# Gate values as four more columns of the value product, a cross product in two row groups, a scan input in two column tiles, and new instruction orders

## The reference

```python
# 1. masked multi-head attention, 16 heads: self (causal), then against ctx, then a small MLP
x1 = layernorm(x + mha(x, x));  x2 = layernorm(x1 + mha(x1, ctx));  x = layernorm(x2 + mlp(x2))
# 2. the pair block: a gate, a cross product, an unscaled self attention
norm_X, norm_F = layernorm(ctx), layernorm(x)
attended = softmax(norm_F @ norm_X.T * scale) @ norm_X
h = gelu(attended @ fc1_w.T + fc1_b)              # 256 -> 4 channels
cross = h @ fc2_w.T + fc2_b                       # 4 -> 256 channels
n = layernorm(cross);  sa = softmax(n @ n.T * scale) @ n
x = norm_F + gamma2 * (cross + gamma1 * sa)
# 3. x = x + softmax(x @ ctx.T) @ ctx
# 4. the mix block: 8-head attention against layernorm(ctx), then a scan over positions
x = x + mha(layernorm(x), layernorm(ctx))
U = (layernorm(x) @ W_in.T + b_in) @ Bmat         # 64 scan channels
s = silu(s @ A.T) + U[t];  x = x + states @ Cmat + mod
```

## Time and profile before

| | |
|---|---|
| median of 3 runs | 4207.41 us (4206.75 to 4208.32) |
| the profiled execution | 4207.95 us, span 4206.2 us |
| PE | 4042.6 us busy (96%) |
| DVE | 3431.2 us (82%) |
| ACT | 3175.7 us (76%) |
| POOL | 2911.0 us (69%) |
| granted clock, mean | 0.989 |

### The profile page before, as it was taken

How to read it: one execution, slowest core, us unless ns; L and a number is a source line. 1 busy time by engine, 2 the same in 40 slices (tenths; PEclk the granted TensorE clock), 3 DMA queues, 4 the chain that set the end, 5 groups by cost and what they waited for, 6 DMA issues and landing times.

```text
span 4206.2 us, 112214 instructions
## 1 busy us (share of the span) xinstructions
PE 4042.6 (96%) x37547; PEld 3383.5 (80%) x37547; DVE 3431.2 (82%) x9517; ACT 3175.7 (76%) x6733; POOL 2911.0 (69%) x3172
## 2 busy tenths in 40 slices
PE   4899999999999999999999999999999999999859
PEld 3688888888888888888888888888888888888645
DVE  3688888888888888888888888888888888888634
ACT  1577887887788778877887787788778877887632
POOL 0477777777777777777777777777777777777634
PEclk9999999999999999999999999999999999999979
DMA  3000100010001100000100010101000000100037
GB/s 108 19 25 25 33 30 28 25 33 30 28 25 33 30 28 26 30 29 27 31 30 28 25 33 30 28 25 33 30 28 26 30 28 25 33 30 25 17 103 272
DMA packets 116547, 159.98 MB, mean 38 GB/s; under 512 B 11350, under 2 KB 103323, under 8 KB 111579
## 3 DMA queue, kind: packets, MB, share of 16 engines
q1 hardware_dynamic: 111626, 146.75, 11.2%
q10 hardware_dynamic: 4368, 6.17, 0.5%
HBM read 115.01 MB, written 37.88 MB: 36 GB/s over the span
## 4 chain that ended last, share of the span: by engine, by line
PE 67%; ACT 12%; POOL 7%; issue 5%; DVE 4%; DMA 0%; ACTq 0%; DVEq 0%; POOLq 0%; SPq 0%
PE bank L674 15%; PE bank L744 9%; PE bank L666 7%; PE bank L682 6%; PE bank L858 4%; PE bank L714 3%; ACT prob L992 3%; PE bank L778 3%; PE bank L693 3%; PE bank L773 2%; POOL rs_ln L1404 2%; PE bank L791 2%; POOL X L1424 2%; POOL X L1418 2%; ACT probT L1002 2%
## 5 line engine op out<-in xcount | busy, mean ns | idle before, releaser
L1158 DVE TENSOR_REDUCE mx<-bank 128x4 f32<-128x512 f32 x1280 | 837.6, 681 | 90.4 <-PE bank L714 68.6
L1169 DVE TENSOR_TENSOR prob<-bank,mx 128x512 f32<-128x512 f32 x1280 | 847.8, 679 | 54.6 <-PE bank L744 33.8
L1002 ACT ACTIVATE probT<-bank 128x512 f32<-128x512 f32 x1280 | 753.3, 600 | 158.9 <-PE bank L778 100.5
L992 ACT ACTIVATE prob<-prob 128x512 f32<-128x512 f32 x1280 | 795.6, 641 | 22.0 <-DVE prob L1169 20.9
L982 ACT ACTIVATE turned<-bank 128x512 f32<-128x512 f32 x896 | 531.9, 616 | 344.0 <-PE bank L666 223.5
L744 PE MATMUL bank<-ident,prob 128*128 128x128 f32 x5120 | 746.3, 277 | 20.3 <-DVE den L1180 6.5
L744 PEld LDWEIGHTS bank<-ident,prob 128*128 128x128 f32 x5120 | 591.3, 142 | 124.9 <-issue 36.8
L674 PE MATMUL bank<-turned,shared 128*128 128x256 f32 x2560 | 605.7, 384 | 1.8 <-ACT turned L982 1.8
L674 PEld LDWEIGHTS bank<-turned,shared 128*128 128x128 f32 x2560 | 468.3, 191 | 69.9 <-issue 14.3
L1404 POOL TENSOR_TENSOR rs_ln<-ve_ln,half 128x2 f32<-128x2 f32 x320 | 226.4, 707 | 384.9 <-DVE ve_ln L1147 384.9
L1483 POOL TENSOR_SCALAR shared<-turned,half_of 128x512 f32<-128x512 f32 x256 | 399.1, 1570 | 79.9 <-ACT turned L982 79.9
(11 more groups left out here) (242 smaller groups left out, 9047.8 us busy)
## 6 DMA issues: line engine op xcount, KB each, us to landing
shared<-in_x SPq DMA_DIRECT2D x128, 256.0 KB, 3.0
CB<-in_ctx SPq DMA_DIRECT2D x64, 256.0 KB, 3.4
CC<-in_ctx SPq DMA_DIRECT2D x64, 256.0 KB, 2.8
mod<-mod_rows SPq DMA_DIRECT2D x64, 256.0 KB, 3.3
residual<-X SPq DMA_DIRECT2D x64, 256.0 KB, 3.5
out<-turned SPq DMA_DIRECT2D x16, 1024.0 KB, 4.8
turned<-residual SPq DMA_DIRECT2D x14, 1024.0 KB, 7.3
u_turned<-us SPq DMA_DIRECT2D x64, 64.0 KB, 2.4
```

What stands on the lines that cost most here:

```text
L992: nc.scalar.activation(flat(t), flat(t), ACT.Exp, scale=SCALE[p]).then_inc(*st["act"].mark(f"exp.{b}{r}"))
L1002: nc.scalar.activation(flat(t), banks.of(f"{att}.turn.{b}{r}")[:, :], ACT.Copy).then_inc(*st["act"].mark(f"probT.{b}{r}"))
L1158: nc.vector.tensor_reduce(m[:], banks.of(f"{att}.tile.{b}{r}")[:, :].rearrange("p (h t) -> p h t", h=4), AX, ALU.max)\
L1169: nc.vector.tensor_tensor(t[:], banks.of(f"{att}.tile.{b}{r}")[:, :].rearrange("p (h t) -> p h t", h=4), maxes.of(f"{att}.max.{b}{r}")[:]. ...
```

## The change

The four gate columns go into the value product: `w_v3` gets 260 columns, of which the last four are `w_gate` scaled by the norm's gain, and the norm's shift goes into the gate's bias once at the start. The step `vx` and its copy are gone; `mix_in.v` is done one round earlier (lag 4), into two banks, and `vp3` has two buffers. DVE divides the probabilities themselves by their sum before `pT1` turns them (`part1`), in place of the two small steps after `av1`. `av1` exchanges its operands, so that its result has the four gate channels on partitions 0 to 3 and 32 to 35; the Gelu reads it from the bank, adds the bias and writes `y5T` directly. `yT` and its copy are gone. `cross` is two products of 32 rows, one per sequence, in two row groups and two banks; ACT copies them with two instructions. `mix_out.u` puts the sequences in two column tiles of 64; SP stores it with two DMAs. PROGRAM and BANKS are written anew for all engines.

The core of the diff (in the kernel after, lines stand 7 to 11 further down):

```diff
-    "pe": """ mix_att.scores.00@6 ctx_att.turn.12@4 ctx_att.values.01@4 ...
+    "pe": """ ctx_att.values.00@4 ctx_att.values.03@4 mix_att.scores.00@6 pair.cross@5 ...
...
-    pair.sc2:2 pair.pT2:6 pair.av:6 real.x4T:2 real.ccT:4 real.screal:4 real.pTreal:4 real.av:5 real.h5T:5
+    ffn.fc2:2 pair.CT:0 pair.FT:2 mix_in.v0:0 mix_in.v1:6 pair.sc1:2 pair.pT1:2 pair.av1:7 pair.cross0:4
...
-        vp3 = sb("vp3", [128, G, D])
+        vp3 = [sb(f"vp3_{n}", [128, G, D + 4]) for n in range(2)]
...
-                def vx(g):
+                def v3(g):
...
+                    took = [banks.claim(f"mix_in.v{b}", mix_in["act"], "v") for b in range(G)]
...
-                            last = nc.tensor.matmul(t[:, b * 4:b * 4 + 4], trn["NXT"][:, a, b * S:(b + 1) * S],
-                                                    w_gate[:, a, :], start=(a == 0), stop=(a == DH - 1))
+                            last = nc.tensor.matmul(t[:, 0:D + 4], trn["HCT"][:, a, b * S:(b + 1) * S], w_v3[:, a, :],
+                                                    start=(a == 0), stop=(a == DH - 1))
...
-                        last = nc.tensor.matmul(t[:, b * 4:b * 4 + 4], pct["1"][:, b, :], vxs[:, b, :], start=True, stop=True)
+                        last = nc.tensor.matmul(t[32 * b:32 * b + 4, 0:S], vp3[g % 2][:, b, D:D + 4], pct["1"][:, b, :], start=True, stop=True)
...
-                        last = nc.tensor.transpose(t[:, b * S:(b + 1) * S], y5[:, b, :], ident[:])
-                    last.then_inc(*pair["pe"].mark("yT"))
...
-                        last = nc.tensor.matmul(t[:, b * D:(b + 1) * D], y5T[:, b, :], w_cross[:], start=True, stop=True)
+                        rows_ = slice(32 * b, 32 * b + 32)
+                        last = nc.tensor.matmul(t[:, 0:D], y5T[rows_, :], w_cross[rows_, :], start=True, stop=True)
...
-                        last = nc.tensor.matmul(t[:, 0:W], w_u[:, a, :], trn["H6T"][:, a, :], start=(a == 0), stop=(a == DH - 1))
+                        for b in range(G):
+                            last = nc.tensor.matmul(t[NS * b:NS * b + NS, 0:S], w_u[:, a, :], trn["H6T"][:, a, b * S:(b + 1) * S],
+                                                    start=(a == 0), stop=(a == DH - 1))
...
-                    nc.scalar.activation(y5[:, :, 0:4], a4[:], ACT.Gelu).then_inc(*pair["act"].mark("gelu"))
+                        last = nc.scalar.activation(y5T[at, :], banks.of("pair.av1")[at, 0:S], ACT.Gelu, bias=gate_col[at, :])
...
+                    for b in range(G):
+                        last = nc.scalar.activation(nat["CR"][:, b, :], banks.of(f"pair.cross{b}")[:, 0:D], ACT.Copy)
...
+                def part1(g):
...
+                        last = nc.vector.tensor_scalar(pc["1"][:, b, :], pc["1"][:, b, :], rsum["1"][:, b:b + 1], None, ALU.mult)
...
-                    sp.dma_start(u_g[g], us[:]).then_inc(u_out.sem, 16)
+                    for b in range(G):
+                        sp.dma_start(u_g[g][b], us[NS * b:NS * b + NS, :]).then_inc(u_out.sem, 16)
```

More of the change, by code:

```diff
@@ L133 @@
     "pe": """
[L134 to L152, removed]
+        ctx_att.values.00@4 ctx_att.values.03@4 mix_att.scores.00@6 pair.cross@5 ctx_att.values.02@4
+        ctx_att.values.01@4 ctx_att.turn.11@4 ctx_att.turn.10@4 ctx_att.back.0@4 mix_in.k@5 ctx_att.turn.13@4
@@ new lines @@
+        ctx_att.turn.12@4 ctx_in.x1T@3 ctx_att.values.11@4 ctx_att.values.13@4 ctx_att.values.10@4
+        ctx_att.values.12@4 real.ccT@5 self_att.causal.00@2 self_att.causal.03@2 mix_att.turn.03@6
+        self_att.causal.01@2 self_att.causal.12@2 ctx_att.back.1@4 self_att.scores.03@2 self_att.scores.01@2
+        self_att.scores.00@2 self_att.scores.12@2 ctx_in.q@3 pair.ncT@5 mix_att.turn.01@6 self_in.len@2 pair.sc2@5
+        mix_att.turn.02@6 mix_att.values.03@6 self_att.causal.10@2 self_att.causal.11@2 self_att.causal.02@2
@@ L153 @@
+        mix_in.v@4 mix_in.q@5 pair.pT1@4 mix_out.u@6 self_in.e0@1 pair.av1@4
     """,
     "act": """
[L155 to L167, removed]
+        pair.HCT@5 ctx_att.exp.02@4 self_in.k@2 pair.FT@5 ctx_att.probT.03@4 ctx_att.probT.00@4 ctx_att.exp.10@4
@@ new lines @@
+        real.h5T@6 pair.exp1@5 ctx_att.exp.11@4 ctx_att.probT.02@4 ctx_att.exp.12@4 mix_in.v@5 pair.pT1@5 mix_in.q@6
+        pair.gelu@5 self_att.ln1@3 pair.cross@5 ctx_att.outT.0@4 ctx_att.exp.13@4 mix_att.exp.03@6
+        ctx_att.probT.10@4 mix_att.exp.01@6 ctx_att.probT.11@4 ctx_att.probT.13@4 ctx_att.probT.12@4 pair.lnN@5
+        ctx_in.x1T@3 ctx_att.outT.1@4 mix_att.exp.02@6 real.ccT@5 mix_att.exp.00@6 mix_att.probT.03@6 pair.ncT@5
+        mix_att.probT.01@6 ctx_in.q@3 mix_att.probT.02@6 pair.exp2@5 ctx_att.ln2@4 pair.pT2@5 mix_att.probT.00@6
@@ L210 @@
-    ctx_att.tile.01:2 ctx_att.tile.02:4 ctx_att.tile.03:1 ctx_att.turn.00:0 ctx_att.turn.01:3 ctx_att.turn.02:2
-    ctx_att.turn.03:1 ctx_att.back.0:2 ctx_att.tile.10:7 ctx_att.tile.11:2 ctx_att.tile.12:1 ctx_att.tile.13:4
-    ctx_att.turn.10:6 ctx_att.turn.11:0 ctx_att.turn.12:6 ctx_att.turn.13:3 ctx_att.back.1:5 ffn.x2T:3 ffn.fc1:4
-    ffn.fc2:2 pair.CT:6 pair.FT:3 pair.vx:0 pair.sc1:3 pair.pT1:7 pair.av1:5 pair.yT:1 pair.cross:5 pair.ncT:2
-    pair.sc2:2 pair.pT2:6 pair.av:6 real.x4T:2 real.ccT:4 real.screal:4 real.pTreal:4 real.av:5 real.h5T:5
```

242 lines of the change are left out of this document (132 added, 110 removed).

## The result

The changed kernel takes 4245.16 us (median of 4 runs, 4244.21 to 4245.91) for 4207.26: ratio 1.0086, 95% interval 1.0074 to 1.0098. It is slower by 38 us; 4168 was forecast, and the time lies above the range. The profiled execution has a span of 4242.4 us, 36.2 more than that of before.

What follows compares the result with a forecast made beforehand. PE's instruction stream was taken to set the 60.67 us round. Per round -2.20 (PE steps) + 0.4 (tiling) + 1.05 (wait for ACT) + 0.1 (smaller waits) = -0.65; over 61 rounds 40 us less: 4168 us, range 4090 to 4222.

Steps and rivals of the forecast that it cites:

- That is 9.65: ACT's summed work from pT1's copy through the ctx probabilities, 9.65 us; it made PE wait 1.05 a round.
- The two Gelus: In ACT's stretch behind pT1: two Gelus of 4 partitions x 128 columns, taken at 0.18 us each.
- The new wait at sc2: Between pair.ncT and pair.sc2 on PE: about 1.05 us of steps left against 1.4 for ACT's copy, +0.3 a round.
- the wait at fc1: On PE, ffn.fc1 stands one transposition nearer to x2T: +0.1 us a round.
- changes of tiling: On PE: about 0.29 us per visit, 8 stretches of tiled steps before and 9 after, taken as +0.4 a round.
- Fill and drain: Some 570 us outside the steady stage: change taken as 0, bounds -10 and +10 us.
- The savings on cross, u and av1: PE per round: cross product -0.44, scan input (u) -0.43, weighted gate values (av1) -0.22 us.
- rivals, 1: PE gets its whole saving because ACT's stretch has slack: -1.8 us a round, 4098 us; chance 0.18.
- Rival 2: Slower: DVE's steps behind the mix scores free PE's banks late; priced at 4235 us; chance 0.14 together with rival 4.
- Rival 4: Each ACT table load also pays a 1.38 us drain, two in the stretch: 4336 us; chance 1 in 100.
- what was to show the forecast right: Signs: gate product gone, cross and scan input about 0.45, period near 60.0, PE waiting about 1 us for ACT, ACT without pause.
- The 0.7 to spare in the old order: ACT has the needed probability tile out at 2573.35, before PE reaches the second ctx values at 2574.02: 0.7 us.

Runs made afterwards that it cites:

- one_gelu: Changed kernel with the second sequence's Gelu left out, one instruction instead of two: 4211.97 us, ratio 1.0010.
- after_half: Changed kernel with half of the mix scores (16 of 32 passes) computed a second time on PE: 4247.08 us, ratio 1.0087.
- before_apart: Old kernel with the last of the four mix values moved behind the transposition pT2, on PE: 4224.66 us, ratio 1.0037.
- values_joined: Changed kernel with the mix values step that stood alone (mix_att.values.03) moved to the other three on PE: 4273.04 us, ratio 1.0153.
- no_tables_dve: Changed kernel with Gelu replaced by identity (no table loads), and DVE centring mix tiles 03 and 01 ahead of CR's statistics: 4215.87 us, ratio 1.0013.
- b2: Changed kernel with the Gelu's table loaded early by a small Gelu and new orders on PE, ACT and DVE: 4291.23 us, ratio 1.0192.
- before_u: Old kernel with one part of the change alone, the scan input in two 64-column tiles: 4207.50 us, ratio 0.9996.
- before_pieces: Old kernel with ACT's copy outT.0 in four pieces of 128 columns: 4220.95 us, ratio 1.0028.
- q_first: Changed kernel with ACT's copies of the mix query ahead of pT1's copy, not behind it: 4264.80 us, ratio 1.0134.
- early_load: Changed kernel with one small extra Gelu of 128x8 constants on ACT ahead of pT1's copy: 4243.75 us, ratio 1.0086.
- no_tables: Changed kernel with the Gelu replaced by an identity with the same bias, so without the two table loads: 4205.40 us, ratio 0.9989.

## Why the prediction was wrong

The mechanism that it named was the right one, and in the right place; two terms of its sum were too small, and the fill was not nothing. Set against the old order the forecast of -0.65 a round is the sum of -0.21 in the stretch (10.25 us from pT1 to the fourth of the second values, where the old order needed 10.46 for the same content) and -0.44 outside. Measured were +0.45 and some +0.05.

1. **The step that failed: "That is 9.65", ACT's content in the stretch.** It is 10.39. The two Gelus take 0.76, not 0.36: no row showed the form, and the value taken near the middle of two rows was below what came, 0.36 busy for each and no overlap. A table load starts 0.02 to 0.04 behind the end of the instruction ahead of it; the sum had let it begin at the distance of two ordinary instructions, 0.09 and 0.13 too early at its two places, though the earlier trace rows show the load 0.03 behind the end of ln1's span. CR's copies start 1.11 behind ln1, not 1.0. Together 0.73 of the 0.74. The fourth values start 10.91 us behind pT1 for 10.25: 0.66 x 61 = 40 of the 77 us by which the forecast was off. one_gelu shows that this term decides (0.50 less on ACT, 33 us), after_half that PE's passes do not.
2. **Outside the stretch, -0.44 for some +0.05: 30 us.** The passes were right (0.81 of the gate product gone, 0.03 added). The new wait at sc2 is 0.3, as forecast, and 0.28 of old waits went, but the wait at fc1 is 0.2 for 0.1 and some small new ones make 0.13, so waits took 0.35 net for 0.1. The rest, some 0.5, is put down to changes of tiling, of which the forecast had 0.24 here. Its count of 8 visits before and 9 after is right. But 3 of the 8 and only 2 of the 9 lie in the stretch, so where PE sets the round there are 7 for 5, and two visits at the 0.27 of before_apart are 0.5; a mix value that stands alone is one of them, some 0.2 (values_joined). This split is read from the distances and the order of the rows, and only single visits were tried by themselves.
3. **Fill and drain, taken as 0 between -10 and +10,** cost 7 us.
4. The savings on cross, u and av1 were sized 0.44, 0.43 and 0.22; the traces show 0.23, 0.29 and about 0.33 (av1's passes run in among those of the values) with their ways out. In the stretch these sizes no longer matter. The sum should have taken the stretch as ACT's row and credited nothing of them; it came out so only because the wait was worked out from what was left.
5. Of the rivals, 1 (PE gets its whole saving) is refuted by the waits. Rival 2 had nearly the time (4235), but not the cause: PE's longest waits name ACT, and DVE's bank costs PE time only where ACT's row was shortened or moved (no_tables_dve, b2). Rival 4 is refuted: both loads here start 0.02 to 0.04 behind the span ahead, and the function follows 0.01 behind the load. "ScalarE: Activation LUTs", What ACT_TABLE_LOAD costs, of the Trainium skill gives a drain of 1.38 us, which this trace does not show. The way in and out of a visit cost the scan input as much as its shorter passes saved (before_u).
6. Of what was to show the forecast right, no gate product, ACT without a pause and waits for y5T and CR of about 1 us a round did show. Cross and scan input at about 0.45 did not (0.64 and 0.58), nor did the period, 61.2 for 60.0.
7. The 0.7 to spare in the old order was read at the second values alone. The copy at 2572.74 is the last of their four tiles, not the last but one, and cross had less to spare, as before_pieces shows. The forecast's sum does not use this figure.

## What to carry to other kernels

A saving counts only where its engine is the bound of that stretch: split the round into stretches, take for each the longest row among the engines that it passes through, and compare those. The cheapest test of where an engine has time to give is to repeat a piece of its work at one place: 0.44 us on PE cost nothing at one place and 26 us at another. In a tight order by hand, a step that looks misplaced may cover a wait, and moving it shows the wait.

## What the runs showed of the hardware

- ACT's function table is loaded when the instruction that needs it has got what it waits for, not ahead of the wait (q_first: 0.58 us idle, then the load of 1.28). A small instruction of the same function, placed where ACT is free, takes the load with it; copies and identities in between do not bring it back (early_load).
- Two Gelus of 4 partitions x 128 columns out of a PSUM bank with a bias per partition, onto partitions 0 to 3 and 32 to 35, take 0.76 us of ACT's row (after), and so do two identities (0.75, no_tables). Each is busy 0.36, and they do not overlap; one alone takes 0.26 (one_gelu), and the 128x8 Gelu out of SBUF 0.12. Why the pair does not overlap is open.
- One more visit of 128-column passes in column tiles costs 0.2 to 0.27 us above its passes (values_joined, before_apart), and for eight passes of 64-column tiles this was all that they saved (before_u).
